# A four-layer convolution and attention network: neighbour mask as constant contraction rows, channel products on GpSimd, the join in three steps, and a new order on every engine

## What is computed

```python
# L0: position attention by a Gram matrix, then a pooled gate
mm1 = softmax(einsum('bci,bcj->bij', x, x)); mm2 = (w_conv @ x) @ mm1
x = gap(x) @ mm2 + x
# L1: q, k of 16 channels, v of 128
attn = softmax(einsum('bci,bcj->bij', q, k)); x = gamma * (v @ attn^T) + x
# L2: neighbour attention (8 neighbours of a pixel) and channel attention (2 neighbours of a channel)
att  = einsum('bkn,bkm->bnm', alpha, sigma)
att  = softmax(where(adj, att, NEG), axis=2);   h_s = att applied to x
Gc   = einsum('bcn,bdn->bcd', x, x)
catt = softmax(where(cadj, Gc, NEG), axis=2);   h_p = catt @ x
x = (1 - gama) * x + gama * elu(h_s + h_p)
# L3: 2-D FFT of 16 projected channels, energy by angle, top 2 peaks, gains, inverse FFT, x + w_out @ ..
```

## Time and profile before

| | us |
|---|---|
| median of 3 runs | 290.47 (290.19 to 290.78) |
| the profiled execution | 290.33 |
| its span, first to last instruction | 288.5 |
| PE busy | 272.3 (94%) in 1499 products |
| DVE busy | 213.2 (74%) |
| ACT busy | 186.2 (65%) |
| POOL busy | 95.1 (33%) |
| PE's share of the chain that ended last | 66% |

### The profile page before, as it was taken

How to read it: one execution, slowest core, us unless ns; L and a number is a source line. 1 busy time by engine, 2 the same in 40 slices (tenths; PEclk the granted TensorE clock), 3 DMA queues, 4 the chain that set the end, 5 groups by cost and what they waited for, 6 DMA issues and landing times.

```text
span 288.5 us, 4440 instructions
## 1 busy us (share of the span) xinstructions
PE 272.3 (94%) x1499; PEld 178.6 (62%) x1499; DVE 213.2 (74%) x325; ACT 186.2 (65%) x355; POOL 95.1 (33%) x102
## 2 busy tenths in 40 slices
PE   7999999999999899999999999799999799999994
PEld 3846555467677576747657464467867557765462
DVE  3865889789998786763489867799788775828383
ACT  0774676789997474766648776688748457674320
POOL 1045031505236878128004101354279814000000
PEclk9999999999999999999999999979999999999998
DMA  6951000000000000000000000000000000000015
GB/s 184 353 202 51 0 1 1 2 0 1 3 0 1 0 2 0 1 3 0 0 3 1 0 2 1 1 0 2 1 0 2 1 0 3 2 4 0 2 73 220
DMA packets 4520, 8.14 MB, mean 28 GB/s; under 512 B 1118, under 2 KB 2014, under 8 KB 4498
## 3 DMA queue, kind: packets, MB, share of 16 engines
q1 hardware_dynamic: 4498, 7.85, 7.8%
HBM read 5.68 MB, written 2.10 MB: 27 GB/s over the span
## 4 chain that ended last, share of the span: by engine, by line
PE 66%; DVE 10%; POOL 8%; ACT 8%; issue 3%; DMA 2%; SPq 1%; DVEq 0%; POOLq 0%; ACTq 0%
PE psum L360 64%; POOL e1h L1047 4%; ACT e L686 3%; DVE e1l L900 3%; DMA qs<-row 2%; ACT psum L677 2%; POOL ks L1040 1%; DVE nmax L884 1%; POOL qs L1037 1%; SPq L348 1%; DVE nmax L850 1%; ACT qs L669 1%; POOL regionb L1010 1%; ACT ks L670 1%; DVE x L860 1%
## 5 line engine op out<-in xcount | busy, mean ns | idle before, releaser
L1047 POOL CAST e1h<-e 128x1024 fp32r<-128x1024 f32 x32 | 42.6, 1333 | 34.7 <-ACT e L686 21.6
L900 DVE TENSOR_TENSOR e1l<-e,e1h 128x1024 fp32r<-128x1024 f32 x32 | 40.8, 1282 | 9.8 <-POOL e1h L1047 9.7
L686 ACT ACTIVATE e<-psum 128x1024 f32<-128x1024 f32 x32 | 32.8, 1025 | 20.6 <-DVE e1l L900 15.7
L850 DVE TENSOR_REDUCE nmax<-psum 128x1 f32<-128x1024 f32 x32 | 39.0, 1221 | 9.3 <-PE psum L360 8.7
L657 ACT ACTIVATE e<-psum,nmax 128x1024 f32<-128x1024 f32 x32 | 35.7, 1115 | 14.2 <-issue 9.6
L884 DVE TENSOR_REDUCE nmax<-psum 128x1 f32<-128x1024 f32 x32 | 38.0, 1217 | 3.9 <-PE psum L360 3.8
L677 ACT ACTIVATE psum<-psum,nmax 128x1024 f32<-128x1024 f32 x32 | 34.8, 1089 | 7.0 <-DVE nmax L884 6.3
L360 PE MATMUL psum<-e,v0n 128*64 128x512 f32 x128 | 31.0, 604 | 0.0
L360 PE MATMUL psum<-ks,qs 96*128 96x512 f32 (+2 forms) x96 | 30.1, 405 | 0.8 <-DVE ks L874 0.4
L360 PE MATMUL psum<-qs,ks 96*128 96x512 f32 (+2 forms) x96 | 28.9, 389 | 1.8 <-DMA qs<-row 1.3
L360 PE MATMUL psum<-xh 128*128 128x512 f32 x64 | 28.3, 442 | 0.6 <-DVE x L860 0.3
(11 more groups left out here) (175 smaller groups left out, 491.4 us busy)
## 6 DMA issues: line engine op xcount, KB each, us to landing
out<-xin SPq DMA_DIRECT2D x8, 256.0 KB, 2.1
xin<-in_x SPq DMA_DIRECT2D x3, 512.0 KB, 6.1
twist<-in_twist_in SPq DMA_DIRECT2D x1, 768.0 KB, 7.4
zz<-in_region_in SPq DMA_DIRECT2D x2, 360.0 KB, 3.5
xin<-in_x SPq DMA_DIRECT2D x2, 256.0 KB, 2.8
untwist<-in_untwist_in SPq DMA_DIRECT2D x1, 512.0 KB, 7.2
...
```

Source lines behind the costliest of these rows:

```text
L686: inc(go(e1[:, E1_AT[b, i], :], t[:, :], ACT.Exp), "e1_ready", b)
L850: inc(vec.tensor_reduce(nmax0[z][:, i:i + 1], t[:, :], AX.X, ALU.max, negate=True), "nmax0_ready", b)
L900: inc(vec.tensor_tensor(e1l[:, EH_AT[b, i], :], e1[:, E1_AT[b, i], :], e1h[:, EH_AT[b, i], :].bitcast(F32), ALU.subtract), "e1l_ready", b)
L1047: done(gp.tensor_copy(e1h[:, EH_AT[b, i], :], e1[:, E1_AT[b, i], :]), "e1h_ready", b, i)
```

## The change

- Neighbour mask. qs and ks get 29 further contraction rows (96 to 124) and a margin of 32 pixels on both sides (NW = 1088 columns). The rows are constants: 27 pairs of indicator rows whose product is -2^53 times a positive number for any pair of pixels in a window that are not neighbours and 0 for neighbours, and two for the margins. near and nearT are now one product of 125 rows and 192 columns per group, without the mask product. The table comes by DMA into e2[1], POOL casts it (nears) into the e1l ring, and four DMAs (nearin, SP) write it into qs and ks of both buffers; the first three e1l steps wait for those. The margins are zeroed by POOL at the start.
- Channel products. Only neighbours c, c+1 are computed: POOL multiplies x2T[c] x2T[c+1] (cprod, 8 x 127 columns) and adds the eight pixel groups in three steps (csum), and PE turns the result into two columns by three fp32 products of 2, 1 and 1 columns. DVE, ACT work on 2 columns; ecn gets two more steps on DVE that put the two columns beside the diagonal.
- Join. joinc (ecT times x2, both halves), joina (pixel groups 0 to 3) and joinb.0, joinb.1 (the rest) replace join.0 and join.1. joinc waits for ecT alone, joina for the first half of e2, joinb for the second. x1 of image b waits only for joinc of image b-2.
- Order. All five lists are new. The 28 warm steps remain; two of them move to the start. regions.0.0 and regions.0.1 move on POOL from between normv.0.2 and split.1, and from between the casts of images 0 and 1, to behind normv.2.1 and split2.3. SP issues region's and nearin's DMAs between the rows.
- Some constants go (identb, nearb, chainb, ones), tiles share space (rws and near in e2), and ACT gets a few waits on buffers of image b-2.

The diff, cut to its core:

```diff
@@ sizes @@
+MASKS = 29
+KS4 = KS3 + MASKS
+NW = N + 2 * W
+NEG = -2.0 ** 53
@@ PE_TEXT, some stretches of the new order @@
...
+    "attL.1.3 near.0.1@2 attL.1.4 attH.1.5 scoreT.1.7@6 attL.1.5 attH.1.6 gram.2.5@0 mix.2.0@6 gram.2.6@2 "
+    "attL.1.6 attH.1.7 gram.2.7@0 attL.1.7 shift2.0.0@2 mix.2.1 asproj.1.0@3 x2T.1.0@4 mix.2.2 nearT.0.0@0 "
+    "chan.0.0@2 mix.2.3 nearT.0.1@4 near.1.0@0 mid.2.0 chanT.0.0@3 mid.2.1 joinc.0.0@4 near.1.1@2 gram.3.0@0 "
+    "joina.0.0 qkproj.2.0@6 joinb.0.0 gram.3.1@2 xconv.3.0@7 gram.3.2@0 joinb.0.1 gram.3.3@2 chan.1.0@6 "
...
+    "near.2.0@0 attL.3.4 near.2.1@6 attH.3.5 attH.3.6 attL.3.5 attH.3.7 attL.3.6 attL.3.7 xturn.1.0@2 chan.2.0@3 "
+    "s1.1.0@2 asproj.3.0@0 shift2.2.0@1 x2T.3.0@6 chanT.2.0@4 joinc.2.0@2 nearT.2.0@4 nearT.2.1@6 near.3.0@0 "
+    "joina.2.0 joinb.2.0 near.3.1@4 joinb.2.1 s2.1.0@6 xproj.2.0@7 chan.3.0@0 xturn.2.0@1 s1.2.0@7 shift2.3.0@2 "
+    "s2.2.0@3 chanT.3.0@4 joinc.3.0@0 nearT.3.0@6 nearT.3.1@4 energy.0.0@2 joina.3.0 joinb.3.0 joinb.3.1 "
+    "selT.0.0@2 warm.0.9@7 warm.0.10@6 region.0.0@2 warm.0.11@7 warm.0.12@6 warm.0.13@5 warm.0.14@7 warm.0.15@6 "
...
@@ ACT, near the end @@
+    "nearT.2.0 nearT.2.1 near.3.0 elu.2.0 elu.2.1 near.3.1 sq.1.0 shift2.3.0 xrow.2.0 xturn.2.0 chan.3.0 s1.2.0 "
+    "sq.2.0 chanT.3.0 mag.0.0 nearT.3.0 nearT.3.1 elu.3.0 elu.3.1 roots.0.0 coefT.0.0 xrow.3.0 xturn.3.0 i1.0.0 "
@@ DVE, near the end @@
+    "near.3.0 elu.2.0 pw.0.0 near.3.1 elu.2.1 zelu.2.0 x3.2.0 zelu.2.1 x3.2.1 shift2.3.0 chan.3.0 ecn.3.0 pw.1.0 "
+    "hart.1.0 pw.2.0 row2.3.0 msum.0.0 pick.0.0 pick.0.1 elu.3.0 selT.0.0 elu.3.1 zelu.3.0 gain.0.0 zelu.3.1 "
+    "x3.3.0 coef.0.0 x3.3.1 coef.1.0 pw.3.0 msum.1.0 hart.2.0 hart.3.0 coef.2.0 pick.1.0 pick.1.1 y.0.0 selT.1.0 "
@@ POOL_STEPS @@
+    "normv.0.0 split.1.0 normv.0.1 split2.1.0 normv.0.2 normv.0.3 normv.1.0 qkdup.0.0 qkdup.0.1 nears.0.0 "
+    "normv.1.1 normv.1.2 normv.1.3 split.2.0 split2.2.0 qkdup.1.0 qkdup.1.1 e1h.0.0 e1h.0.1 e1h.0.2 e1h.0.3 "
+    "e1h.0.4 e1h.0.5 e1h.0.6 e1h.0.7 e1h.1.0 e1h.1.1 e1h.1.2 asdup.0.0 e1h.1.3 asdup.0.1 e1h.1.4 xkeep.0.0 "
+    "e1h.1.5 e1h.1.6 normv.2.0 e1h.1.7 cprod.0.0 normv.2.1 regions.0.0 csum.0.0 normv.2.2 normv.2.3 asdup.1.0 "
+    "asdup.1.1 split.3.0 cprod.1.0 split2.3.0 regions.0.1 csum.1.0 qkdup.2.0 qkdup.2.1 normv.3.0 normv.3.1 "
+    "xkeep.1.0 normv.3.2 normv.3.3 qkdup.3.0 qkdup.3.1 e1h.2.0 e1h.2.1 e1h.2.2 e1h.2.3 e1h.2.4 e1h.2.5 e1h.2.6 "
+    "e1h.2.7 e1h.3.0 e1h.3.1 e1h.3.2 e1h.3.3 e1h.3.4 asdup.2.0 asdup.2.1 e1h.3.5 cprod.2.0 e1h.3.6 e1h.3.7 "
+    "csum.2.0 asdup.3.0 asdup.3.1 cprod.3.0 xkeep.2.0 csum.3.0 xkeep.3.0")
@@ SP @@
+    "regin.0.0 row1.0.0 nearin.0.0 row1.1.0 regin.0.1 row2.0.0 row2.1.0 row1.2.0 row1.3.0 row2.2.0 row2.3.0")
+                if name == "nearin":
+                    wait(sp, "nearr_ready", 0)
+                    for k in range(2):
+                        for n, dst in enumerate((qs, ks)):
+                            sp.dma_start(dst[k][KS3:KS4, :].bitcast(F32),
+                                         nearr[n * G:n * G + MASKS, :].bitcast(F32)).then_inc(near_sem, 16)
@@ PE: chan @@
-                    for u in range(CH):
-                        mm(t[:, 0:P], x2T[z][:, u, :], x2T[z][:, u, :], u == 0, False)
-                    end(step, mm(t[:, 0:P], identb[:], chainb[:], False, True))
+                    mm(t[:, 0:2], ident, edge[:], True, False, True)
+                    mm(t[:, 0:1], cgram[:, 0:P], one[:], False, False, True)
+                    end(step, mm(t[:, 1:2], cgram[:, 1:P + 1], one[:], False, True, True))
@@ PE: near and nearT @@
-                        mm(t[:, w0:w0 + WIN], identb[:], nearb[:, kind, :], first, False, True)
-                        last = mm(t[:, off:off + hi - lo], lhs[:, u * P:(u + 1) * P], rhs[:, lo:hi],
-                                  False, not first, True)
+                        last = mm(t[:, w0:w0 + WIN], lhs[:, W + u * P:W + (u + 1) * P], rhs[:, u * P:u * P + WIN],
+                                  True, True)
@@ DVE: e1l @@
+                    if EH_PRIOR[b, i] is None:
+                        dve.wait_ge(near_sem, 16 * 4)
@@ POOL @@
+                elif name == "cprod":
+                    wait(pool, "x2T_ready", b)
+                    settle()
+                    done(gp.tensor_tensor(prod[:], x2T[z][:, :, 0:P - 1], x2T[z][:, :, 1:P], ALU.mult), "cgram_ready", b)
+                elif name == "csum":
+                    if b:
+                        pool.wait_ge(filled[BANK["chan", b - 1, 0]], NTH["chan", b - 1, 0])
+                    for n, k in enumerate((4, 2, 1)):
+                        settle()
+                        to = prod[:, 0:k, :] if k > 1 else cgram[:, 1:P].unsqueeze(1)
+                        done(gp.tensor_tensor(to, prod[:, 0:k, :], prod[:, k:2 * k, :], ALU.add), "cgram_ready", b, n + 1)
```

More of the change, by code:

```diff
@@ L155 @@
     near=lambda i: [("sum1_ready", CH + 4 * i + 3)], nearT=lambda i: [("e2_ready", i)],
-    join=lambda i: [("zelu_ready", 1)], xproj=lambda i: [("xrow_ready", 0)], xturn=lambda i: [("a1_ready", 0)], s1=lambda i: [("s1_ready", 0)],
+    joinc=lambda i: [("zelu_ready", 1)], xproj=lambda i: [("xrow_ready", 0)], xturn=lambda i: [("a1_ready", 0)], s1=lambda i: [("s1_ready", 0)],
     s2=lambda i: [("hart_ready", 0)], energy=lambda i: [("es_ready", 0)], selT=lambda i: [("selT_ready", 0)],
@@ L160 @@
 ONE_BANK = "warm gap xconv qkproj asproj chan chanT xproj xturn s1 s2 energy selT region coefT i1 i2 shift1 shift2".split()
-SHARES = dict(mix=("mix", 0), mid=("mix", 0), attH=("attH", 0), attL=("attH", 0), join=("join", 0), wout=("wout", 0))
+SHARES = dict(mix=("mix", 0), mid=("mix", 0), attH=("attH", 0), attL=("attH", 0), joinc=("joinc", 0), joina=("joinc", 0), joinb=("joinc", 0), wout=("wout", 0))
 def banks():
@@ L216, in conv_seq @@
         xrow = sb("xrow", [P, 2 * P])
-        ident = sb("ident", [P, P])
-        chain = sb("chain", [P, P])
+        beside = sb("beside", [P, P + 2])
+        ident, above, below = beside[:, 1:P + 1], beside[:, 0:P], beside[:, 2:P + 2]
+        edge = sb("edge", [P, 2])
+        one = sb("one", [P, 1])
         turn = sb("turn", [P, 2 * P])
@@ L265, in conv_seq @@
         nmaxc, sumc, recc = two("nmaxc", [P, 1]), two("sumc", [P, 1]), two("recc", [P, 1])
-        ec, ecn, ecT = two("ec", [P, P]), two("ecn", [P, P]), two("ecT", [P, P])
+        prod = sb("prod", [P, CH, P - 1])
+        cgram = sb("cgram", [P, P + 1])
+        ec, ecw, ecu = two("ec", [P, 2]), two("ecw", [P, 2]), two("ecu", [P, P])
+        ecn, ecT = two("ecn", [P, P]), two("ecT", [P, P])
         e2 = two("e2", [P, CH, WIN])
+        near = e2[1][0:2 * G].rearrange("p u w -> p (u w)")[:, 0:NW]
+        nearr = e1l[0:2 * G].rearrange("p r n -> p (r n)")[:, 0:NW]
+        rws = e2[0][:].rearrange("p u w -> p (u w)")[:, 0:3 * P].rearrange("p (k c) -> p k c", c=P)
         zz = sb("zz", [P, N])
-        near = zz[:, 0:3 * WIN].rearrange("p (k w) -> p k w", w=WIN)
         region = zz[0:NBINS, :].rearrange("p (j c) -> p j c", c=P)
@@ L501, in _ @@
                     t = begin(step)
-                    end(step, nc.tensor.transpose(t[:, 0:P], ecn[z][:], ident[:]))
+                    end(step, nc.tensor.transpose(t[:, 0:P], ecn[z][:], ident))
                 elif name in ("near", "nearT"):
@@ L522, in _ @@
-                    end(step, last)
-                elif name == "join":
-                    if i == 0:
-                        wait(pe, "ecT_ready", b)
-                        wait(pe, "e2_ready", b, 1)
-                        begin(step)
-                    t = tile(step)
-                    mm(t[:, hc], ecT[z][:], x2[z][:, hc], True, False, True)
-                    for u in range(CH):
-                        lo = max(u * P - W, i * HALF)
-                        hi = min((u + 1) * P + W, (i + 1) * HALF)
-                        if lo < hi:
-                            off = lo - (u * P - W)
-                            last = mm(t[:, lo:hi], x2T[z][:, u, :], e2[z][:, u, off:off + hi - lo],
-                                      False, u * P + P + W >= (i + 1) * HALF and u in (4, 7), True)
-                    inc(last, "join_full", b)
+                        last = mm(t[:, w0:w0 + WIN], lhs[:, W + u * P:W + (u + 1) * P], rhs[:, u * P:u * P + WIN],
+                                  True, True)
@@ new lines, in _ @@
+                    end(step, last)
+                elif name == "joinc":
+                    wait(pe, "ecT_ready", b)
+                    t = begin(step)
+                    for h in range(2):
+                        ho = slice(h * HALF, (h + 1) * HALF)
+                        last = mm(t[:, ho], ecT[z][:], x2[z][:, ho], True, False, True)
+                    inc(last, "join_chan", b)
+                elif name in ("joina", "joinb"):
+                    wait(pe, "e2_ready", b, int(name == "joinb"))
+                    t = tile(step)
```

(33 more changed lines are left out.)

171 lines of the change are left out of this document (93 added, 78 removed), and 141 rows, old and new, of tables (ACT_STEPS, DVE_STEPS, PE_TEXT, POOL_STEPS).

## The result

The changed kernel takes 313.27 us (median, 311.39 to 316.20) against 290.54 of the kernel before: a ratio of 1.076, 95% interval 1.068 to 1.085. It is 7.6% slower (the ratio leaves out the execution at 316.20, which ran in a slower state); forecast were 281.8 us. The profiled execution took 311.66 us.

A forecast was written before the change was run, and what follows sets the result against it. PE bounds 120 to 180 us, PE, DVE and ACT together 60 to 80, the order of short steps the end. Gains 0 + 4.2 + 0.8 + 3.2 + 0.5 = 8.7 us gave 281.8 us on the median, range 277 to 288.5.

The forecast's parts named there:

- Part 4: The four mask-row transfers behind row1.0's two: they end at 71.6 to 72.8 us and cost nothing to 1 us.
- Part 1: Mask products leave near and nearT: 64 times 0.105 us, 6.7 us of PE saved.
- rival B: Mask product was hidden in the data product's weight load, saving 0.04 instead of 0.105 us each: 285 us, chance 0.12.
- rival F: Instructions go, but the new order turns freed time into waits for DVE or ACT: 290.3 us, chance 0.04.
- (a) to (c): Gains over 60 to 234.8 us, in order: 0; 4.2 us (111 to 180 us, after 1.5 charged for POOL); 0.8 us.
- Part 2: chan shrinks from 1.84 to 0.66 us an image: 4.7 us of PE saved.
- rival C: POOL bounds 115 to 150 us: 286 us, chance 0.17; sign: PE or PEld waits over 1.5 us for v0n or xl.
- Part 5 (c): 180 to 234.8 us: near.2 gives 0.8 us; xkeep.2 leaving and cprod.2 entering image 3's casts give nothing.
- Part 3: POOL's new products and sums: 20.8 us over four images, 1.5 charged; DVE's two added ecn steps at most 0.8 us.
- Rival E: POOL's products and DVE's two-input operations block each other, seen at e1l and the casts: slower, 292.2 us, chance 0.09.
- Part 5 (d): Last x2 to last x3: to shift2.3 10.2 becomes 10.7 us, from there 18.5 becomes 14.8: 3.2 us gained.
- (e): End of the kernel: energy.1 no longer waits for a wout half, 0.5 us gained.

The follow-up runs named there:

- e1: The changed kernel with 32 rows instead of 29 in each of the four mask-row transfers (three more hold zeros): 296.24 us.
- e11: e3 with GpSimd's product and sums of the second image (cprod.1, csum.1) placed later, behind split2.3 and regions.0.1: 290.56 us.
- e7: e5 with 14 warm-up products on PE ahead of xproj.2, as in e3: 288.08 us.
- e6: The kernel before with only the mask rows new (32-row transfers issued at 30 us), old order and old channel part: 288.65 us.
- e14: e7 with four more filler products ahead of the first scoreT of image 2, written to PSUM bank 1: 287.36 us.
- e15: e11 with four more filler products ahead of the first scoreT of image 2, written to the free PSUM bank 1: 289.73 us.
- e5: e1 with the channel products on PE as in the kernel before, without cprod and csum, new order kept: 290.53 us.
- e8: e5 with PE's shift2.3 and chan.3 ahead of xproj.2 again, as before the change, DVE's and ACT's steps to match: 294.06 us.
- e3: e1 with 14 warm-up products (no reader) on PE ahead of xproj.2: 293.25 us.

## Why the prediction was wrong, point by point

Starts in us of the second half of three DVE steps, and the span; "forecast" moves the kernel before by the prediction's terms:

| kernel | x1 of image 3 | x2 of image 3 | x3 of image 3 | span |
|---|---|---|---|---|
| before | 180.1 | 234.0 | 267.8 | 288.5 |
| forecast | 175.9 | 229.0 | 259.6 | 279.8 |
| after | 195.7 | 252.8 | 288.9 | 309.8 |
| e1, 32 rows | 178.9 | 236.2 | 273.9 | 294.7 |
| e11, whole change mended | 176.6 | 233.2 | 267.7 | 288.6 |
| e7, old channel products | 176.2 | 230.2 | 263.3 | 284.1 |

**Part 4 is the step that failed first, by 17 us of time.** I took the landing of the mask rows at "1.8 to 3 us" from the row's own transfer of another shape and concluded "Nothing to 1 us". The landing was 20.7 us behind the last issue, and DVE stood 17.9 us for it. The sum of the issues (69.2 against my 69.8) was right. No row of before has a transfer of 29 partitions, and I carried the time over from one of another first dimension. With 32 rows the very estimate holds: 2.7 to 2.8 us.

**Part 1 held as a price and failed as a gain.** 0.11 to 0.13 us a product instead of 0.22 a pair was measured, so rival B (0.18) is out. But the mask alone brought 1.7 us (e6): in the old order most of the freed time turned into waits, as rival F (0.04) had it for the new one. In the new order, with the old channel products and the clock held, (a) to (c) brought 234.0 - 230.2 = 3.8 us (2.6 in e14, with a fall of the clock at 189.3). Of my 5.0, 2.4 were chan's and 1.5 a charge for POOL, so without these 4.1 were forecast.

**Part 2 held as a price (0.67 us) and is a loss on the whole.** The products' version is 2.4 us over the other (e15 and e14) where the sum had 0.9 of gain, 2.4 less the charge of 1.5 in (b). In my walk for images 0 and 1, csum.0 ended 1.8 us later than I had it (in e1 9.0 us behind e1h.1.7 instead of 7.2), still 4 us ahead of PE's chan.0. Nor did rival C come: in e1 PEld stands 1.2 us in all for POOL's v0n, under the 1.5 of its sign. What I hadn't walked was cprod.1 beside ecn, cprod.2 between the casts of image 3 and csum.2 in front of chan.2. The "nothing" for cprod.2 among the casts, in Part 5 (c), is one term: it cost 1.8 us, and 1.3 more in front of chan.2 (e11). And where I put "at most 0.8 us" for what DVE gets (Part 3), ecw and ecn took 3.8 us in e1.

**Rival E had the mechanism, at 0.09, and not the place.** I looked for it at e1l and the casts. Its sign, an e1l median well over 1.3 us or maxima over 3, didn't show: 1.22 and 2.06 in e1. It struck ecw and ecn, whose product PE waits for with nothing else to do. The Trainium skill (SBUF — State Buffer, section "SBUF: two separate sides") has the rule: GpSimd and some of DVE's operations share a pair of ports, and whichever starts first holds it for the whole instruction. e1 and e11 agree with it: each of the four held DVE steps starts 0.2 to 0.5 us behind the start of a POOL step and ends within 0.2 us of its end.

**Part 5 (d) was mis-sized.** From x2 to x3 of image 3 I forecast 30.6 us instead of 33.8. With PE at the full clock it is 33.1 (e7), in e11 34.5, in e1 37.7. The term was 3.2 and is 0.7 at best. What failed is the first half of the walk: from nearT.2 to shift2.3 I had 10.7 us, and it is 12.7 in e11 and 13.1 in e7, for PE stands for x3 of image 2 in front of xproj.2 (2.7 us in e5, 3.9 in e1), a wait that I had not in my walk. The second half, to the end of x3, was 14.8 and is 14.3 in both. e8 shows that the old order of PE's tail is 3.5 us slower with these parts, so the change of order isn't what failed. (e) was 0.5 and is -0.1 (from x3 to the end 20.7 us before, 20.8 in e7).

**The clock was in no term.** The kernel before has 3.4 us at the half clock behind 180 us (187.6 to 191.0). Of e1's loss against the forecast (296.2 against 281.8) 3.0 us are shown to be the clock behind xproj.2 (e3), 2.7 the product beside ecn with the fall of the clock that follows it (e11), and 2.4 to 3.2 the rest of the channel products (e15 against e14, e11 against e14). 5.6 us remain between e14 and the forecast. Of them 2.5 are (d), 0.6 are (e), and 0.9 the net of chan, which e14 doesn't have. The other 1.6 I can't place; e14 still has 3.4 us at the half clock in its profile. Were Part 4 the only failure, e1 would have come out near 281.8; it came out at 296.2, above the whole range, and so did e15, at 289.7 against 288.5.

The new order (with e7's fillers or without) is worth 1.5 to 2.8 us where PE keeps its clock (e7's lower cluster at 286.0 to 287.1 and e5's 285.8 against e6's 288.65), and less than nothing in e5's other executions (290.3 to 291.7).
